# A fused two-layer transformer kernel: batch 0's routing moved forward, the expert steps split into five kinds, and batch 1's second bias formed on VectorE

## The chip, the cores and the metric

The program runs on one core of one Trainium2 chip. The metric is the device time of one execution in microseconds (us); lower is better. The kernel before takes 197.06 us, the median of three runs.

## The reference

Two samples (batches) of 512 tokens with 128 features pass through two cross-attention layers and two mixture-of-experts layers:

```python
x = x + L0_xcond(layernorm(x), ctx, ctx, tau, delta)   # 16 heads, 77 keys
x = x + L0_ffn(layernorm(x))                           # one shared FFN + an expert's LoRA
x = x + L1_xcond(layernorm(x), ctx, ctx, tau, delta)
x = x + L1_ffn(layernorm(x))                           # top-1 of 8 experts

def _L1_ffn_ref(x, switch_w, switch_b, w1, b1, w2, b2):
    t = x.reshape(-1, d)
    route_prob = softmax(t @ switch_w + switch_b)
    route_prob_max = max(route_prob); routes = argmax(route_prob)
    for e in range(8):
        h = gelu(t @ w1[e] + b1[e])          # 128 -> 512
        y = h @ w2[e] + b2[e]                # 512 -> 128
        out = where(routes == e, y, out)
    return out * route_prob_max
```

The change is in the last layer and in what leads up to it.

## The kernel before

The order of the work is written out by hand. `schedule()` (L107) holds a table of steps such as `sc/1/1/3` (kind / layer / batch / number), and each of the five engines walks through the same list and issues its own part of every step. So a step's place in the table sets its place in each engine's queue, and each engine runs its queue strictly in order; semaphores tie the engines together.

Steps that matter here:
- Attention: `max` (TensorE scores of a group, VectorE takes the row maximum, L965 and L756), `mt` (the maxima are transposed, L974, and copied by ScalarE and VectorE, L612 and L762), `sc` (scores on TensorE, L990, exponential on ScalarE, L620), `pv` (times the values, L1005), `rd` and `on` (reciprocal of the denominator on ScalarE, product on VectorE, L766), `wo` (output projection, L1012, and residual add on VectorE, L775).
- Routing of one batch: `ln/3` and `xn/3` (statistics and normalized rows, L690 to L708; in the last layer the reciprocal root is a `pow` on GpSimd, L500), `xt/3` (transposes, L917, and copy by ScalarE, L579), `route` (gate product, L1025, and the arg-max chain on VectorE, L786 to L796), `prob` (L810 to L816), `rank` (L1062, L1067; VectorE L841 to L850 gives each token its slot), `tiles` (L855 to L859, the expert of each tile, `tile_e`).
- GpSimd then scatters the batch's rows to the DRAM buffer `slots`, sorted by expert, with four indirect DMAs (L534). SyncE waits for all four and loads them back as 11 tiles of 128 rows in four DMAs (`LOADS`, L431).
- Expert steps: 22 tiles, 11 for each batch. In step `moe/t` TensorE transposes tile t+1 (L1091), forms the hidden layer of tile t (L1098, called H below) and the output of tile t-2 (L1109, called Y). ScalarE copies the transposed tile (`XST`, L659) and applies gelu (L666). VectorE copies the first weights of tile t+2's expert into one of `NWC` = 3 buffers (L871, called the weight copy: H of a tile waits for it), adds the gated second bias to tile t-1 (L879) and the result to tile t-2 (L884, called z). GpSimd forms the gated bias of a tile (`bias_of`, L479 to L492, buffer `PB`) and stores tile t-2 to `out` with an indirect DMA (L542).

Between the end of attention and the first tile TensorE runs `BRIDGE_X` = 14 products of constants (`keep_busy`, L903), whose result is not used. In the table `xt/3/1`, the transposes of batch 1, follows `moe/-1`, the transpose of tile 0:

```python
xn/3/1 moe/-1 xt/3/1 moe/0 route/1 moe/1 prob/1 rank/1 tiles/1
...
return steps + [("moe", t) for t in range(2, NS + 2)]
```

Of the kernel before, what the change touches and what calls it, by code (L numbers as in the profile page):

```python
# [57 lines left out]
NSB = NQ + E - 1  # L58
NS = B * NSB
# [5 lines left out]
BRIDGE_Q, BRIDGE_X = 14, 14  # L65
NHB = 3
NWC = 3
NPB = 6
AHEAD = NQ
# [37 lines left out]
def schedule():  # L107
# [50 lines left out]
def banks(steps):  # L158
# [22 lines left out]
def build(nc, x, ctx, att0, att1, consts, small, rows, ffn0w, loraB, sw, w1, b1, w2, b2, empty, out):  # L181
# [8 lines left out]
    with stages:  # L190
# [243 lines left out]
        def _(pool):  # L434
# [44 lines left out]
            def bias_of(n):  # L479
# [7 lines left out]
                if n >= NPB:  # L487
                    pool.wait_ge(based, n - NPB + 1)
# [3 lines left out]
                pool.tensor_tensor(PB[:, n % NPB], B2[:, bass.ds(e * D, D)], p, ALU.mult).then_inc(bias_ready, 1)  # L492
# [3 lines left out]
            for s in steps:  # L496
                if s[0] == "ln" and s[1] == 3:
                    b = s[2]
                    pool.wait_ge(var_ready, b + 1)
# [23 lines left out]
                elif s[0] == "rank":  # L523

                    b = s[1]
                    if b == 1:
                        bias_of(0)
                    pool.wait_ge(preset, 16)
                    pool.wait_ge(slot_ready, b + 1)
                    pool.wait_ge(p_ready, b + 1)  # L530
                    for i in range(b * NQ, (b + 1) * NQ):
                        if b == 1 and i > NQ:
                            bias_of(i - NQ)
                        pool.indirect_dma_start(slots, bass.IndirectOffsetOnAxis(ap=slot[:, i:i + 1], axis=0), ROW[:, i], None,  # L534
                                                bounds_check=NS * 128 - 1, oob_is_err=False).then_inc(rows_sent[b], 16)
                elif s[0] == "moe" and s[1] >= 2:

                    t = s[1] - 2
                    if t + AHEAD < NS:
                        bias_of(t + AHEAD)  # L540
# [671 lines left out]
```

## Time and profile before

| | us |
|---|---|
| median of 3 runs (197.03 to 198.96) | 197.06 |
| the profiled execution's own time | 196.75 |
| its span, first to last instruction | 194.9 |
| TensorE matmuls busy | 164.1 (84%) |
| VectorE busy | 122.1 (63%) |
| ScalarE busy | 97.4 (50%) |
| GpSimd busy | 75.5 (39%) |
| share of the chain that ended last: TensorE / VectorE / issue | 56% / 20% / 9% |

The profile comes from one execution of 196.75 us, whose span is 194.9 us. 1.85 us of its time lie around the span. Times in the trace count from the span's start. "Busy" for TensorE is the modelled time of its pipelined matmuls. The granted clock is given as a share of 2.4 GHz: 0.50 is the level of 1.2 GHz. What each engine waited for is in brackets behind a row.

### The profile page before, as it was taken

How to read it: one execution, taken by the hardware profiler on the slowest of the kernel's cores; microseconds unless marked ns; L12 is line 12 of the kernel's file. 1: busy time of each engine (PE TensorE's matmuls, PEld its weight loads, DVE VectorE, ACT ScalarE, POOL GpSimd, SP SyncE). 2: the span in 40 equal slices, each digit the busy share in tenths (PEclk: the TensorE clock that was granted, in tenths of full speed). 3: DMA queues.
4: the chain of work that ended last, by engine and by line, in shares of the span. 5: the costliest groups of instructions: out<-in, count | busy, mean ns of one | idle time of the engine just before them, and what ended most of it. 6: DMA issues, size and time to landing. Idle time of an engine off the chain costs nothing.

```text
span 194.9 us, 3393 instructions
## 1 busy us (share of the span) xinstructions
PE 164.1 (84%) x880; PEld 112.7 (58%) x881; DVE 122.1 (63%) x360; ACT 97.4 (50%) x228; POOL 75.5 (39%) x96
## 2 busy tenths in 40 slices
PE   7894699989988978678897989995678999999930
PEld 2542555646735733454573455633367999999920
DVE  2689845859663559977433998374567666655420
ACT  5392427845562363452327554465255576766700
POOL 8899160000400066020002001016204889888871
PEclk9999669999999999999999999999999999999996
DMA  6400007000000599940000000002640273100000
GB/s 189 159 3 4 4 5 246 6 0 3 5 4 7 143 330 405 531 171 0 3 0 0 0 0 0 0 3 97 180 138 31 82 194 123 32 18 10 22 26 2
DMA packets 14483, 15.48 MB, mean 79 GB/s; under 512 B 6842, under 2 KB 11205, under 8 KB 14400
## 3 DMA queue, kind: packets, MB, share of 16 engines
q1 hardware_dynamic: 12944, 13.29, 21.2%
q0 software_dynamic: 1088, 1.60, 2.5%
q10 hardware_dynamic: 432, 0.37, 0.7%
q8 instruction: 8, 0.13, 0.3%
q14 instruction: 11, 0.09, 0.2%
HBM read 13.50 MB, written 5.44 MB: 97 GB/s over the span
## 4 chain that ended last, share of the span: by engine, by line
PE 56%; DVE 20%; issue 9%; ACT 4%; POOL 4%; DMA 3%; POOLq 0%; SPq 0%; ACTq 0%; DVEq 0%
PE acc L1005 10%; PE scores L1098 9%; PE acc L1109 8%; PE scores L990 4%; PE shared L1052 4%; DVE MR L756 4%; DVE QG L746 4%; PE shared L965 3%; PE acc L903 3%; PE shared L1038 3%; PE shared L945 3%; POOL out L542 2%; PE shared L917 2%; PE shared L1025 2%; DVE XN L708 2%
## 5 line engine op out<-in xcount | busy, mean ns | idle before, releaser
L1005 PE MATMUL acc<-P,VP 123*128 123x512 f32 (+1 forms) x80 | 41.6, 620 | 0.6 <-ACT P L620 0.6
L620 ACT ACTIVATE P<-scores 123x512 f32<-123x512 f32 (+1 forms) x40 | 23.0, 595 | 22.3 <-PE scores L990 21.9
L666 ACT ACTIVATE HT<-scores,B 128x128 f32<-128x128 f32 x88 | 25.3, 369 | 12.7 <-PE scores L1098 10.0
L756 DVE TENSOR_REDUCE MR<-shared 128x4 f32<-128x308 f32 x64 | 26.8, 471 | 4.9 <-PE shared L965 4.5
L522 POOL TENSOR_TENSOR X<-X,ROWS 128x512 f32<-128x512 f32 x6 | 8.1, 1345 | 52.4 <-DVE XN L708 52.2
L990 PE MATMUL scores<-QG,KG 102*123 102x512 f32 (+1 forms) x48 | 23.1, 530 | 2.6 <-ACT QG L612 1.2
L542 POOL DMA_INDIRECT out<-XS,token x22 | 22.7, 1031 | 4.2 <-issue 4.0
L1098 PE MATMUL scores<-XST,HT 128*128 128x128 f32 x176 | 23.6, 277 | 0.8 <-ACT XST L659 0.8
L965 PE MATMUL shared<-KG,QG 98*128 98x308 f32 x64 | 21.5, 399 | 3.0 <-DVE MR L756 1.1
L1109 PE MATMUL acc<-W,HT 128*128 x176 | 23.1, 276 | 0.2 <-issue 0.2
L1098 PEld LDWEIGHTS scores<-XST,HT 128*128 128x128 f32 x176 | 21.4, 192 | 1.3 <-ACT XST L659 1.2
L1109 PEld LDWEIGHTS acc<-W,HT 128*128 128x128 f32 x176 | 21.3, 192 | 0.4 <-issue 0.4
L1005 PEld LDWEIGHTS acc<-P,VP 123*128 123x128 f32 (+1 forms) x80 | 14.6, 197 | 9.7 <-issue 7.4
L965 PEld LDWEIGHTS shared<-KG,QG 98*128 98x128 f32 x64 | 11.8, 195 | 11.3 <-issue 3.7
L746 DVE SCALAR_TENSOR_TENSOR QG<-shared,ATT,QG 32x512 fp32r<-32x512 f32 x16 | 11.9, 745 | 7.5 <-ACT QG L605 7.2
L871 DVE COPY HT<-W 128x512 f32 x22 | 10.2, 465 | 8.8 <-issue 7.4
L534 POOL DMA_INDIRECT slots<-ROW,slot x8 | 8.4, 1049 | 18.1 <-DVE slot L850 8.7
L513 POOL TENSOR_TENSOR KG<-Ks,CON 102x616 fp32r<-102x616 f32 x6 | 7.5, 1250 | 18.7 <-DVE Ks L723 18.3
L605 ACT ACTIVATE QG<-shared,ATT 64x512 fp32r<-64x512 f32 x16 | 10.9, 684 | 6.1 <-PE shared L945 5.8
L990 PEld LDWEIGHTS scores<-QG,KG 102*123 102x123 f32 (+1 forms) x48 | 8.4, 190 | 8.5 <-issue 5.4
L903 PE MATMUL acc<-idle 128*128 128x512 bf16 x40 | 11.8, 459 | 1.5 <-DVE idle L681 1.4
L492 POOL TENSOR_TENSOR PB<-B,XS 128x128 f32<-128x128 f32 x22 | 10.2, 465 | 2.7 <-issue 2.1
(121 smaller groups left out, 238.8 us busy)
## 6 DMA issues: line engine op xcount, KB each, us to landing
W<-in_w SPq DMA_DIRECT2D x16, 256.0 KB, 6.8
slots<-in_empty SPq DMA_DIRECT2D x1, 2860.0 KB, 14.2
XS<-slots SPq DMA_DIRECT2D x2, 650.0 KB, 6.1
XS<-slots SPq DMA_DIRECT2D x2, 390.0 KB, 4.2
W<-in_ffn0w SPq DMA_DIRECT2D x1, 534.0 KB, 4.5
XS<-slots SPq DMA_DIRECT2D x2, 260.0 KB, 2.7
X<-in_x SPq DMA_DIRECT2D x2, 256.0 KB, 4.1
B<-in_b SPq DMA_DIRECT2D x1, 512.0 KB, 4.3
```

The lines of the kernel that those rows point to most:

```text
L542: pool.indirect_dma_start(out, bass.IndirectOffsetOnAxis(ap=token[:, t:t + 1], axis=0), XS[:, t, 0:D], None, bounds_check=B * S - 1, oob_i ...
L605: act.activation(QG[0:64, b, g], bank(s)[r, :], ACT.Identity, bias=ATT[l][r, A_BQ + g:A_BQ + g + 1]).then_inc(qh_ready, 1)
L620: act.activation(P[0:w, n % NP], scores[n % 2][0:w, :], ACT.Exp).then_inc(probs_ready, 1)
L666: ins = act.activation(HG1[:, t % NHB, c], hidden[t % 2][:, c], ACT.Gelu_apprx_tanh, bias=B1[:, bass.ds(expert[t] * NF + k, 1)])
L746: dve.scalar_tensor_tensor(QG[64:96, b, g], bank(s)[64 * odd:64 * odd + 32, :], ATT[l][0:32, A_BQ + g:A_BQ + g + 1], QG[0:32, b, g].bitcas ...
L756: dve.tensor_reduce(MR[:, b, qt, g, 2:2 + HG], bank(s)[:, 0:GK].rearrange("p (h k) -> p h k", h=HG), AX.X, ALU.max).then_inc(max_read, 1)
L903: pe.matmul(acc[0][:, :], idle[:, 0:128], idle[:, 0:S], start=True, stop=True)
L965: pe.matmul(bank(s)[:, 0:GK], QG[0:ONES + 2, b, g, 128 * qt:128 * qt + 128], KG[0:ONES + 2, b, g, off:off + GK], start=True, stop=True).th ...
L990: ins = pe.matmul(scores[n % 2][0:w, :], KG[:, b, g, c:c + w], QG[:, b, g], start=(i == 0), stop=(i == len(parts) - 1))
L1005: pe.matmul(acc[half][:, :], VP[0:w, l, b, j, half], P[0:w, n % NP, :], start=(j == 0), stop=(j == NT - 1)).then_inc(probs_used, 1)
L1098: ins = pe.matmul(hidden[t % 2][:, 128 * k:128 * (k + 1)], W1C[:, t % NWC, 128 * k:128 * (k + 1)], XST[:, t % 2], start=True, stop=True)
L1109: ins = pe.matmul(acc[n % 2][:, 0:D], HG1[:, n % NHB, 128 * k:128 * (k + 1)], W2[:, bass.ds(expert[n] * (NF * D) + D * k, D)], start=(k == ...
```

## The change

The table of steps is rewritten from batch 1's second attention layer on, and the step `moe` is split into kinds with places of their own: `cw` (weight copy), `m1` (transpose of the next tile, H, gelu), `bs` (second bias), `m2` (Y and z), `pb` (bias formed on GpSimd) and `so` (store). `row` is one of the scatters that belonged to `rank`; `prob` has become the first part of `rank` on VectorE.

```diff
-NWC = 3
-NPB = 6
-AHEAD = NQ
+NPB = NSB
+NWC = 4
-BRIDGE_Q, BRIDGE_X = 14, 14
+BRIDGE_Q, BRIDGE_X = 14, 0
...
-        xn/3/1 moe/-1 xt/3/1 moe/0 route/1 moe/1 prob/1 rank/1 tiles/1
+        pv/1/1/9 rd/1/1/1 on/1/1/1 wo/1/1 m1/-1 pb/0:3 ln/3/1 m1/0 cw/2 m1/1 xn/3/1 bs/0 cw/3 m1/2 m2/0 xt/3/1 pb/3:6
+        bs/1 m1/3 so/0 route/1 cw/4 m2/1 pb/6 bs/2 rank/1 so/1 tiles/1 pb/7 m1/4 row/1/0 pb/8 row/1/1 pb/9 row/1/2 pb/10
+        row/1/3 m2/2 bs/3 cw/5
...
-    return steps + [("moe", t) for t in range(2, NS + 2)]
+    for t in range(5, NS + 3):
+        steps += [(kind, n) for kind, n in (("cw", t + 1), ("m1", t), ("bs", t - 1), ("m2", t - 2), ("pb", t + 4), ("so", t - 3))
+                  if n < NS and (kind != "pb" or NSB <= n < NPB)]
+    return steps
```

`NSB` is 11, so `NPB` = 11 means that GpSimd forms the gated bias for batch 0's tiles only. For batch 1 VectorE multiplies and adds in one instruction:

```diff
+                    if n < NPB:
                         dve.wait_ge(bias_ready, n + 1)
-                        dve.tensor_tensor(XS[:, n, 0:D], XS[:, n, 0:D], PB[:, n % NPB], ALU.add).then_inc(based, 1)
+                        dve.tensor_tensor(XS[:, n, 0:D], XS[:, n, 0:D], PB[:, n], ALU.add).then_inc(based, 1)
+                    else:
+                        dve.scalar_tensor_tensor(XS[:, n, 0:D], B2[:, bass.ds(expert[n] * D, D)], XS[:, n, R_P:R_P + 1],
+                                                 XS[:, n, 0:D], ALU.mult, ALU.add).then_inc(based, 1)
```

Batch 0's last reciprocal root goes from GpSimd's `pow` to ScalarE's Ln and Exp, as in the earlier layers; batch 1's stays on GpSimd:

```diff
-                if s[0] == "ln" and s[1] == 3:
+                if s == ("ln", 3, 1):
                     b = s[2]
-                    pool.wait_ge(var_ready, b + 1)
+                    pool.wait_ge(var_ready, 1)
...
-                    if st == 3:
+                    if (st, b) == (3, 1):
                         continue
```

**Batch 0's chain on TensorE**, from the second `mt` step of batch 1's attention to `route/0` (the gate product, L1025). Before:

```order
L974 MATMUL shared<-CON,MR 64x128 x4
L990 MATMUL scores<-QG,KG 123x512
L1005 MATMUL acc<-P,VP 128x512
L990 MATMUL scores<-QG,KG 123x512 x2
L1005 MATMUL acc<-P,VP 128x512
L990 MATMUL scores<-QG,KG 123x512
L917 MATMUL shared<-CON,ROW 128x128 x4
L1005 MATMUL acc<-P,VP 128x512
L1025 MATMUL shared<-SW,XNT 128x8 x4
```

Now:

```order
L917 MATMUL shared<-CON,ROW 128x128 x4
L1005 MATMUL acc<-P,VP 128x512
L965 MATMUL shared<-KG,QG 128x308 x2
L990 MATMUL scores<-QG,KG 123x512
L974 MATMUL shared<-CON,MR 64x128 x4
L1025 MATMUL shared<-SW,XNT 128x8 x4
```

The transposes of batch 0 (L917) have moved in front of `mt` (L974); `route/0` directly follows `mt`, and two `sc` and one `pv` that stood ahead of it come after it.

**The start of the expert steps on TensorE**, from batch 1's output projection (L1012). Before, with the bridge (L903) and batch 1's transposes (L917) right behind tile 0's (L1091):

```order
L1012 MATMUL shared<-ATT,OT 128x128 x4
L903 MATMUL acc<-idle 128x512 x14
L1085 TENSOR_LOAD tile_e
L1085 ISA x2
L1091 MATMUL shared<-CON,XS 128x128
L917 MATMUL shared<-CON,ROW 128x128 x4
```

Now:

```order
L1012 MATMUL shared<-ATT,OT 128x128 x4
L1083 TENSOR_LOAD tile_e
L1083 ISA x2
L1089 MATMUL shared<-CON,XS 128x128
L1083 TENSOR_LOAD tile_e
L1083 ISA x2
L1089 MATMUL shared<-CON,XS 128x128
L1096 MATMUL scores<-XST,HT 128x128 x4
```

The bridge is gone. Four tile transposes (L1089), three H (L1096) and the first Y now stand ahead of batch 1's transposes.

**VectorE at the end of batch 1's `tiles` step** (the last instruction writes `tile_e`). Before:

```order
L859 TENSOR_SCALAR tile_e<-tile_f 1x11
L868 TENSOR_LOAD tile_e
L868 ISA x2
L871 ISA
L871 COPY HT<-W 128x512
```

Now:

```order
L855 TENSOR_SCALAR tile_e<-tile_f 1x11
L884 SCALAR_TENSOR_TENSOR XS<-acc,XS 128x128
L873 CAST token<-XS 128x3
L876 TENSOR_TENSOR XS<-XS,PB 128x128
L864 TENSOR_LOAD tile_e
L864 ISA x2
L867 ISA
L867 COPY HT<-W 128x512
```

Before, the copy behind `tile_e` is tile 4's weights; now tile 4's copy stands ahead of `rank/1`, and behind `tile_e` come tile 2's z, tile 3's bias and then tile 5's weight copy.

On GpSimd the `pow` for batch 1 (`ln/3/1`) now stands behind `pb/0`, `pb/1` and `pb/2`, which wait for the first two loads; the four scatters of batch 1 have `pb/8` to `pb/10` between them where three other bias steps stood; and in the loop only stores are left.

## Rows read from the trace of the kernel before

**Rows 1.** windows of six stretches, columns in the first row.

```profile
core 0: us, PE busy (x) PEld busy (x) DVE busy (x) ACT busy (x) POOL busy (x), PEclk, DMA share, GB/s
14.00:20.50 6.50, 3.72 (x19) 2.18 (x17) 6.40 (x16) 1.62 (x1) 5.83 (x6) 1.00 0.07 4
20.50:27.30 6.80, 5.62 (x12) 2.85 (x11) 4.67 (x15) 2.17 (x5) 1.60 (x2) 0.50 0.07 5
66.00:71.00 5.00, 3.73 (x13) 1.79 (x12) 4.08 (x16) 3.60 (x8) 1.03 (x1) 1.00 0.96 279
131.60:139.40 7.80, 4.10 (x21) 2.26 (x22) 3.79 (x15) 2.50 (x3) 4.18 (x5) 1.00 0.34 107
139.40:152.56 13.16, 11.15 (x88) 9.79 (x89) 8.74 (x38) 7.75 (x28) 3.77 (x6) 1.00 0.36 112
152.56:186.66 34.10, 34.09 (x304) 33.90 (x303) 20.38 (x61) 22.45 (x84) 30.16 (x40) 1.00 0.23 67
```

**Rows 2.** timeline, batch 0's chain: start us, us, what, [idle before it <-releaser].

```profile
116.50 1.13 PE L1012 MATMUL shared<-ATT,OT 128*128 128x128 f32 x8
...
122.02 1.12 DVE L708 TENSOR_SCALAR ROW<-ROW,mean_var,rstd 128x128 f32<-128x128 f32 x4 [0.58 <-POOL rstd L500]
...
125.82 0.19 DVE L786 TENSOR_TENSOR lg<-shared,ROWS 128x32 f32<-128x32 f32 x1 [2.69 <-PE shared L1025]
```

**Rows 3.** chain that ended last, two pieces of TensorE's work in batch 1's attention.

```profile
120.77 0.86 PE acc L1005 x2
...
121.93 0.47 PE scores L990
```

**Rows 4.** timeline, end of attention to the first expert tile, TensorE and SyncE.

```profile
133.71 1.13 PE L1012 MATMUL shared<-ATT,OT 128*128 128x128 f32 x8 [2.16 <-DVE OT L766]
...
134.89 2.97 PE L903 MATMUL acc<-idle 128*128 128x512 bf16 x13
...
137.18 1.86 SPq L431 DMA_DIRECT2D XS<-slots  x4
...
139.40 0.33 PE L1091 MATMUL shared<-CON,XS 128*128 128x128 f32 x1 [1.54 <-DMA XS<-slots]
```

**Rows 5.** timeline, start of the expert phase, TensorE, ScalarE and GpSimd.

```profile
139.66 0.63 PE L917 MATMUL shared<-CON,ROW 128*128 128x128 f32 x4
...
139.77 0.28 ACT L659 ACTIVATE XST<-shared 128x128 f32<-128x128 f32 x1 [5.62 <-PE shared L1091]
...
140.38 0.41 POOL L492 TENSOR_TENSOR PB<-B,XS 128x128 f32<-128x128 f32 x1 [2.09 <-issue]
...
140.57 1.13 PE L1098 MATMUL scores<-XST,HT 128*128 128x128 f32 x8
...
141.54 0.96 PE L1025 MATMUL shared<-SW,XNT 128*128 128x8 f32 x8
...
141.85 1.14 ACT L666 ACTIVATE HT<-scores,B 128x128 f32<-128x128 f32 x4 [0.67 <-PE scores L1098]
```

**Rows 6.** timeline, VectorE from batch 1's routing to tile 4's weights.

```profile
142.53 0.19 DVE L786 TENSOR_TENSOR lg<-shared,ROWS 128x32 f32<-128x32 f32 x1 [0.57 <-PE shared L1025]
...
148.59 0.16 DVE L859 TENSOR_SCALAR tile_e<-tile_f 1x11 int32<-1x11 f32 x1
...
149.35 0.43 DVE L871 COPY HT<-W 128x512 f32 x1 [0.60 <-DVE tile_e L859]
```

**Rows 7.** timeline, TensorE at tiles 5 and 11, SyncE at batch 1's loads.

```profile
152.56 1.12 PE L1098 MATMUL scores<-XST,HT 128*128 128x128 f32 x8
...
156.45 1.85 SPq L431 DMA_DIRECT2D XS<-slots  x4
...
161.99 0.27 PE L1091 MATMUL shared<-CON,XS 128*128 128x128 f32 x1
```

**Rows 8.** timeline, the last result on VectorE and the last store on GpSimd.

```profile
186.94 0.35 DVE L884 SCALAR_TENSOR_TENSOR XS<-acc,XS 128x128 f32<-128x128 f32 x1 [0.79 <-PE acc L1109]
...
189.82 0.97 POOL L542 DMA_INDIRECT out<-XS,token  x1 [0.30 <-issue]
```

More of the change, by code:

```diff
@@ L152, in order @@
         nth[s] = counts[kind] = counts.get(kind, -1) + 1
-        if s[0] == "ln" and s[1] < 3:
+        if s[0] == "ln" and s[1:] != (3, 1):
             nth["act_ln", s[1], s[2]] = counts["act_ln"] = counts.get("act_ln", -1) + 1
@@ L165, in banks @@
         kind = s[0]
-        if kind == "moe":
+        if kind == "m1":
             rotation = 2
@@ L522, in _ @@
                     finish(pool.tensor_tensor(X[:, b], X[:, b], row, ALU.add), pre_added)
[L523 to L540, printed above, removed]
+                elif s[0] == "row":
+                    _, b, i = s
+                    if i == 0:
+                        pool.wait_ge(preset, 16)
+                        pool.wait_ge(slot_ready, b + 1)
+                        pool.wait_ge(p_ready, b + 1)
+                    i += b * NQ
+                    pool.indirect_dma_start(slots, bass.IndirectOffsetOnAxis(ap=slot[:, i:i + 1], axis=0), ROW[:, i], None,
+                                            bounds_check=NS * 128 - 1, oob_is_err=False).then_inc(rows_sent[b], 16)
+                elif s[0] == "pb":
+                    bias_of(s[1])
+                elif s[0] == "so":
+                    t = s[1]
                     pool.wait_ge(z_ready, t + 1)
@@ L836, in _ @@
                     b = s[1]
+                    dve.wait_ge(ex_ready, b + 1)
+                    if b == 1:
+                        link(dve.tensor_scalar(ex[:, b], ex[:, b], -1.0, 1.0, ALU.mult, ALU.add))
+                        link(dve.reciprocal(ex[:, b], ex[:, b]))
+                    link(dve.tensor_reduce(esum[:, b], ex[:, b], AX.X, ALU.add))
+                    if b == 1:
+                        link(dve.tensor_scalar(esum[:, b], esum[:, b], 2.0, -float(E), ALU.mult, ALU.add))
+                    dve.wait_ge(rows_set, 1)
+                    dve.reciprocal(ROW[:, b * NQ:(b + 1) * NQ, R_P], esum[:, b]).then_inc(p_ready, 1)
                     read(dve, s)
@@ L1070, in _ @@
                     ins.then_inc(full[use[s][0]], 1)
-                elif kind == "moe":
+                elif kind == "m1":
                     t = s[1]
                     if t == -1:
-                        for e in range(E):
-                            pe.wait_ge(in_w2[e], 16)
                         for i in (2, 3):
```

100 lines of the change are left out of this document (44 added, 56 removed).

## The prediction

> **What bounds the kernel now.** I read the windows first, because the kernel has stages with different limits. From 152.56 us to 186.66 us TensorE is busy for 34.09 of 34.10 us [rows 1]: this stage is TensorE's own work, 17 H and 19 Y groups and the transposes of tiles 7 to 21, and it shrinks only if something is taken from TensorE. Nothing is. So the change can gain or lose at three places: before 152.56, in the clock, and behind 186.66.
>
> The timeline shows those places. Batch 0's chain comes first: output projection on TensorE at 116.50, normalized rows on VectorE at 122.02 after GpSimd's `pow`, logits on VectorE at 125.82 [rows 2]. TensorE finishes attention at 134.84, fills 2.97 us with the bridge, and still waits 1.54 us for the first load before tile 0 at 139.40 [rows 4]. From there to H of tile 5 at 152.56 it is busy 11.15 of 13.16 us [rows 1, 7]. At the end VectorE writes the last z at 187.29 (186.94 + 0.35), but the last store starts at 189.82 [rows 8], because GpSimd is behind with its stores.
>
> **Batch 0's chain.** TensorE's output projection waited for VectorE, which had two row maxima and a copy ahead of the product; now the product comes first, and the reciprocal root no longer goes through GpSimd. So the normalized rows may come up to 2.7 us earlier than 122.02. But they are not what `route/0` waits for last: `mt` of the last maxima now stands right in front of it, and all TensorE work ahead of that. What has left the queue ahead of `route/0` is two `sc` at 0.47 and one `pv` at 0.86 [rows 3], 1.8 us; I expect about 0.9 us of new gaps there (TensorE waits for the product on VectorE, then the third `sc` waits for the first exponential). That leaves 0.9 us, between 0 and 2.7. All that follows (rank, scatters, SyncE's loads from 137.18 on [rows 4]) is a chain of its own and shifts with it. **Tile 0 is at 138.5 instead of 139.40.** TensorE's attention ends near 134.84 as before: the same products, and the two new weight copies on VectorE fit in its wait for the last reciprocal.
>
> **From tile 0 to H of tile 5.** This is the term I trust most, for it comes from the order. Before, batch 1's transposes came 0.26 us after tile 0's (139.40 to 139.66 [rows 4, 5]). Now three H and one Y stand ahead of them. Leg by leg:
> - tile 0 to its H, 139.40 to 140.57 [rows 4, 5]: 1.17
> - H to gelu, 140.57 to 141.85: 1.28. Then gelu 1.14 and the copy of tile 2's transpose 0.28, which ScalarE does in that order [rows 5], less 0.1 of overlap: 1.3
> - H of tile 2 and Y of tile 0: 34.10 us for 36 groups [rows 1] is 0.95 each, 1.9
> - batch 1's transposes to `route/1`, 139.66 to 141.54 [rows 5]: 1.9, with one H in it as before
> - `route/1` to the logits on VectorE, 141.54 to 142.53 [rows 5, 6]: 1.0
> - logits to the end of `tile_e`, 142.53 to 148.75 [rows 6]: 6.2, plus one z at 0.35 [rows 8]: 6.5. Tile 4's weight copy is in it as before
> - `tile_e` to H of tile 5. Before, the weight copy started 0.60 us later and took 0.43 [rows 6], 1.1 with the semaphore. Now one z, a cast and a bias add, small operations like the z, precede it, about 0.8 more: 1.9.
>
> The sum is 1.17 + 1.28 + 1.3 + 1.9 + 1.9 + 1.0 + 6.5 + 1.9 = 16.9 us, against 13.16. H of tile 5 starts at 138.5 + 16.9 = 155.4, which is **2.8 us later** than 152.56. TensorE has nothing to do in between: Y of tile 2 ends near 151.4 and H of tile 5 is next in its queue, held by the weight copy behind `tile_e`. That is a new wait of some 4 us. `pow` for batch 1, now behind three bias steps on GpSimd, is a parallel path: the first bias started 0.98 us after tile 0's load (139.40 to 140.38 [rows 4, 5]), so three end some 2.9 us after it, the rows follow about 2.2 us later, at 143.6, and TensorE comes to the transposes at 144.2. It is hidden by 0.6 us; if GpSimd takes longer for each, up to 1 us more is lost.
>
> After H of tile 5 everything is as before, one group behind the other. Batch 1's loads start at 156.45 [rows 7] plus the shift of `tile_e` (4.8 us), 161.3, and tile 11 is there 2.2 us later, as tile 0 was (137.18 to 139.40 [rows 4]), at 163.5; TensorE wants it at 161.99 [rows 7] + 2.8 = 164.8. It fits, by 1.3 us.
>
> **The stores.** GpSimd no longer forms 11 biases, 0.41 us each [rows 5] plus issue, so it keeps up. The last store then starts 0.7 to 1.5 us after the last z instead of 2.53 us (187.29 to 189.82 [rows 8]); it can't be at once, since three results come closer together than three stores of 0.97 us plus 0.30 can go [rows 8]. **Gain 1.5 us**, between 1.1 and 1.9. VectorE's combined instruction costs what a z costs, 0.35 us, a little more than the add; VectorE is busy 20.38 of 34.10 us [rows 1], so that is hidden. If it were not, 11 times 0.1 us would be lost.
>
> **The clock.** TensorE's granted clock is 1.00 in the stretch with the bridge [rows 1]. It fell to 0.50 (1.2 GHz) at 20.5 us after TensorE had been busy for 3.72 of 6.50 us, and came back at 27.3, after 5.62 us of busy time at the low level. With 3.73 of 5.00 us busy, at 66 to 71, it stayed up [rows 1]. Without the bridge TensorE does 1.13 us [rows 4] in the 6.9 us from 131.6 to 138.5. That is far below the stretch after which it fell, and so is the 4 us wait before tile 5. I expect the low level twice.
> - Before tile 0: what TensorE does in the path up to batch 1's transposes is 0.33 + 1.13 + 1.9, 3.4 us. All of it at half speed costs 3.4 more, none of it 0. Part of the low time passes while TensorE waits for ScalarE anyway; I take 1.2.
> - Before tile 5: there TensorE is the bound, and what is lost is half of the busy time at the low level, at most 5.62 / 2 = 2.8, at least 0. I take 1.3, since the low level will have begun in the wait.
>
> The Trainium skill says the same of such waits ("TensorE: Matmul & The Clock Gate", section "HAM oscillation — how this bites in real kernels"): a burst of matmuls, a wait for a transfer, and the next burst starts at half clock, each time anew. By it alone the sum would have both falls for certain, and a kernel that takes the bridge out loses by it. The trace agrees that the clock falls after sparse stretches, but the stretch at 66 to 71 us shows that not each wait does it.
>
> **The sum.** 2.8 (tile 5 later, which has the 0.9 of batch 0's chain in it) - 1.5 (stores) + 1.2 + 1.3 (clock) = +3.8 us. The span goes from 194.9 to 198.7 and the execution from 196.75 to 200.6. The profiled execution lies 0.3 us below the median of the runs; I leave that out. I predict 200.6 us.
>
> **Rivals.**
> - *The clock stays up, or falls at no cost.* Then only 2.8 - 1.5 = +1.3 is left: 198.1 us. For it: a low stretch can coincide with the wait. Against it: 1.13 us of work in 6.9.
> - *Faster: batch 0's loads land when attention ends.* If the first load is there by 134.9, TensorE goes on without a wait, the clock stays up, and H of tile 5 is at 134.9 + 16.9 = 151.8, 0.8 earlier than before; with the stores that is -2.3, 194.4 us. It needs batch 0's chain 4.5 us shorter; with the clock at no cost the kernel is faster than before once tile 0 is earlier than 138.5 - 1.3 = 137.2. The rows show 2.7 us at most for the normalized rows, and `route/0` has TensorE's queue in front. But my gaps are estimates, and a shorter chain also takes the clock's cost away.
> - *Batch 1 is late twice.* If `pow` and the bias steps take 1 us more and both falls cost most of their bounds, it is 200.6 + 1 + 1.5, about 203 us; tile 11 also comes too late once its 1.3 us are used up.
> - *GpSimd's relief is worth nothing*, because the last store waits for something else than GpSimd: then +1.5, 202.1 us. Against it: the stores at the end follow one another at 1.27 us without waiting for VectorE.
>
> **How the numbers follow.** A measurement of this kernel tells about 1% from no change, so faster is below 195.1 and slower above 199.0. The forecast has a chance of 0.45; the clock rival 0.27; the faster one 0.17; the two late ones 0.11 together. The forecast and the late ones are slower, 0.55 with a little taken off for a cheap clock; the clock rival is the same, 0.28; faster 0.17. The forecast's own range is 199 to 202.5. For 8 in 10 the range goes from 195.5, which leaves most of the faster case out, to 203.
>
> **What would show it.** Right: tile 0's transpose at 138 to 139 with an idle TensorE since 135, granted clock 0.50 right behind it; TensorE waiting 3 to 5 us for VectorE's weight copy of tile 5, at about 151 to 155; the last store 0.7 to 1.5 us after the last z. Wrong: tile 0 before 137, no wait at tile 5, or clock 1.00 throughout. The prediction as a whole is wrong if H of tile 5 starts before 153.

## The result, and the profile after

The changed kernel takes **203.26 us** (median of 4 runs, 202.73 to 205.04) against 197.05 us for the kernel before in the same session: ratio **1.032, interval 1.024 to 1.040**. It is slower by 6.2 us. The direction was forecast; the size was not: 200.6 had been said, and 203.26 lies just above the range, whose upper end was 203.0. A second session (run a0 below) gave 203.12 us and 1.036 (1.030 to 1.042). Below, a median is taken over all executions of a kernel, a ratio only over those within 1.5% of its fastest, which leaves out up to two of four (e3, e4, e11) and four of ten (h1).

The profiled execution is the slowest of the four: 205.04 us, span 202.9. This is the head of its page, with the row of the clock from its table of 40 slices:

```profile
span 202.9 us, 3306 instructions
PEclk9997579999999997999999999995899699999995
```

Each digit of PEclk is some 5 us. The 5 two thirds along the row (137 to 142 us) and the 6 behind it (157 to 162) are the two falls of the clock that the prediction wanted. The 7 before the middle (near 80 us) is a fall that neither the profile of before nor a0's has. It lies ahead of all the steps that were changed, and by 116 us this execution is 1.1 us behind a0's. The windows, in stretches that answer to [rows 1], show it in numbers:

```profile
131.60:139.60 8.00, 5.31 (x17) 2.99 (x15) 1.96 (x4) 3.70 (x5) 3.38 (x4) 0.82 0.32 101
139.60:156.60 17.00, 12.25 (x89) 11.10 (x89) 10.96 (x52) 8.17 (x29) 7.70 (x13) 0.88 0.23 73
156.60:196.00 39.40, 37.40 (x303) 35.78 (x303) 17.49 (x57) 22.74 (x83) 21.67 (x24) 0.96 0.21 65
```

From tile 0's transpose (139.6) to H of tile 5 (156.6) are 17.0 us; the prediction had 16.9, and 1.2 more for the clock; before it was 13.16. The surprise is the last row: 39.4 us for work that took 34.10 us before [rows 1]. The timeline of the end of attention, tile 0 and tile 5 answers to [rows 4 to 7]; its columns are start, duration, engine, line and operation, and in brackets the idle time before it with its releaser:

```profile
137.02 2.05 PE L1012 MATMUL shared<-ATT,OT 128*128 128x128 f32 x8 [2.16 <-DVE OT L765]
...
137.38 1.86 SPq L435 DMA_DIRECT2D XS<-slots  x4
...
139.62 0.48 PE L1089 MATMUL shared<-CON,XS 128*128 128x128 f32 x1 [0.56 <-DMA XS<-slots]
...
155.03 0.16 DVE L855 TENSOR_SCALAR tile_e<-tile_f 1x11 int32<-1x11 f32 x1
...
155.95 0.54 DVE L867 COPY HT<-W 128x512 f32 x1 [0.23 <-issue]
...
156.59 1.46 PE L1096 MATMUL scores<-XST,HT 128*128 128x128 f32 x8 [3.22 <-issue]
...
162.81 1.85 SPq L435 DMA_DIRECT2D XS<-slots  x4
```

The output projection of batch 1, the end of attention, starts at 137.02 instead of 133.71 [rows 4], of which 1.2 us are there before 116 us already, and runs at the low clock. H of tile 5 waits 3.22 us for the weight copy at 155.95, as forecast. Batch 1's tile numbers are 6.4 us later than before (155.03 against 148.59 [rows 6]), its loads too (162.81 against 156.45 [rows 7]).

Behind that comes what the prediction did not have. The stores of tiles 2, 3 and 4 (GpSimd, L541) go out with nothing between them, and the engines that read TensorE's results start long after these are recorded as done:

```profile
161.57 0.97 POOL L541 DMA_INDIRECT out<-XS,token  x1 [0.30 <-issue]
...
162.09 1.06 PE L1096 MATMUL scores<-XST,HT 128*128 128x128 f32 x8
...
162.85 0.97 POOL L541 DMA_INDIRECT out<-XS,token  x1 [0.30 <-issue]
162.98 1.06 PE L1108 MATMUL acc<-W,HT 128*128 x8
...
164.12 0.97 POOL L541 DMA_INDIRECT out<-XS,token  x1 [0.30 <-issue]
...
166.13 1.15 ACT L665 ACTIVATE HT<-scores,B 128x128 f32<-128x128 f32 x4 [3.28 <-PE acc L1108]
166.19 0.35 DVE L884 SCALAR_TENSOR_TENSOR XS<-acc,XS 128x128 f32<-128x128 f32 x1 [2.34 <-PE acc L1108]
...
167.50 0.70 PE L1096 MATMUL scores<-XST,HT 128*128 128x128 f32 x4 [1.46 <-ACT XST L658]
```

By the record H of tile 7 ended at 163.15 and Y of tile 5 at 164.04. ScalarE starts the gelu of tile 7 at 166.13, 2.98 us after the one, and VectorE z of tile 5 at 166.19, 2.15 us after the other; both engines were idle, and by the profile both waited for TensorE. Later it repeats in small. In steady state before, z started 0.11 us behind its Y. Now each second z is 0.7 us late:

```profile
171.43 0.97 POOL L541 DMA_INDIRECT out<-XS,token  x1 [1.74 <-DVE XS L884]
...
172.56 1.06 PE L1108 MATMUL acc<-W,HT 128*128 x8
172.81 0.99 POOL L541 DMA_INDIRECT out<-XS,token  x1 [0.41 <-issue]
...
174.38 0.35 DVE L884 SCALAR_TENSOR_TENSOR XS<-acc,XS 128x128 f32<-128x128 f32 x1 [1.43 <-PE acc L1108]
```

Y ends at 173.62, z starts at 174.38; two stores, 1.38 us apart, precede it. (Two z close together also bring the next two stores close together, so here the pairs are effect as well as possible cause.) The next weight copy is late by as much, the next H waits 0.2 to 0.3 us, and two tiles take 4.08 us instead of 3.79 (H of tile 11 at 171.60, of tile 13 at 175.68).

At the end the stores do keep up as forecast: last z at 196.01 + 0.35, last store at 197.85, 1.5 us later instead of 2.53:

```profile
196.01 0.35 DVE L884 SCALAR_TENSOR_TENSOR XS<-acc,XS 128x128 f32<-128x128 f32 x1 [0.62 <-PE acc L1108]
...
197.85 0.98 POOL L541 DMA_INDIRECT out<-XS,token  x1 [0.30 <-issue]
```

### The profile page after: what moved, and what is told of

Its sections match the earlier page's. It is cut to its first block and busy times, and to the rows that moved or that the text cites. A ratio compares the mean times of both kernels' runs of the same rounds, so it can differ in the third digit from the quotient of the medians.

```text
span 202.9 us, 3306 instructions
## 1 busy us (share of the span) xinstructions
PE 167.7 (83%) x867; PEld 117.5 (58%) x867; DVE 120.4 (59%) x359; ACT 98.8 (49%) x230; POOL 67.6 (33%) x84
## 5 line engine op out<-in xcount | busy, mean ns | idle before, releaser
L1096 PE MATMUL scores<-XST,HT 128*128 128x128 f32 x176 | 26.0, 295 | 5.3 <-issue 3.4
L541 POOL DMA_INDIRECT out<-XS,token x22 | 21.8, 993 | 23.7 <-DVE XS L884 18.5
L1096 PEld LDWEIGHTS scores<-XST,HT 128*128 128x128 f32 x176 | 23.4, 207 | 7.4 <-issue 5.2
L965 PE MATMUL shared<-KG,QG 98*128 98x308 f32 x64 | 23.1, 432 | 3.9 <-DVE MR L755 1.9
L990 PE MATMUL scores<-QG,KG 102*123 102x512 f32 (+1 forms) x48 | 24.0, 546 | 1.3 <-ACT P L619 0.8
L1108 PE MATMUL acc<-W,HT 128*128 x176 | 23.9, 283 | 0.0
L1108 PEld LDWEIGHTS acc<-W,HT 128*128 128x128 f32 x176 | 22.2, 198 | 0.0
L965 PEld LDWEIGHTS shared<-KG,QG 98*128 98x128 f32 x64 | 12.9, 213 | 12.5 <-issue 6.8
L884 DVE SCALAR_TENSOR_TENSOR XS<-acc,XS 128x128 f32<-128x128 f32 x22 | 7.6, 348 | 17.2 <-PE acc L1108 13.3
L903 PE MATMUL acc<-idle 128*128 128x512 bf16 x27 | 8.9, 501 | 1.4 <-DVE idle L680 1.4
```

The lines of the kernel that those rows point to most:

```text
L541: pool.indirect_dma_start(out, bass.IndirectOffsetOnAxis(ap=token[:, t:t + 1], axis=0), XS[:, t, 0:D], None, bounds_check=B * S - 1, oob_i ...
L965: pe.matmul(bank(s)[:, 0:GK], QG[0:ONES + 2, b, g, 128 * qt:128 * qt + 128], KG[0:ONES + 2, b, g, off:off + GK], start=True, stop=True).th ...
L990: ins = pe.matmul(scores[n % 2][0:w, :], KG[:, b, g, c:c + w], QG[:, b, g], start=(i == 0), stop=(i == len(parts) - 1))
L1096: ins = pe.matmul(hidden[t % 2][:, 128 * k:128 * (k + 1)], W1C[:, t % NWC, 128 * k:128 * (k + 1)], XST[:, t % 2], start=True, stop=True)
L1108: ins = pe.matmul(acc[n % 2][:, 0:D], HG1[:, n % NHB, 128 * k:128 * (k + 1)], W2[:, bass.ds(expert[n] * (NF * D) + D * k, D)], start=(k == ...
```

## The experiments

Times are medians; ratios are to the kernel before on the same chip, with their interval. A shift of one microsecond between single profiled executions means nothing: the low-clock stretch near 20 us varies in length (the mean granted clock of the first 40 us is 0.91 or 0.87), and some executions have a second one near 80 us. So I compare places within one execution, or two executions that are equally far at 115 us.

**a0: the changed kernel again.**

> The changed kernel once more, unaltered, to see which of its waits stand in every execution. If the long wait of tile 5 (TensorE idle 3.2 us behind tile 5's transpose), the low clock at 137 to 143.5 and at 157 to 160.5, and the 1.5 us wait of H of tile 9 for ScalarE at 166 to 167.5 come from the order, all of them are there again, each within 0.5 us. If the wait at tile 9 came from one disturbed execution, it is gone and the time is about 201.5 us. Time: 202.7 to 203.6 us.

203.12 us, 1.036 (1.030 to 1.042). Its profiled execution (span 200.5) is without the fall near 80 us (granted clock 1.00 from 78 to 82 us, 0.59 in the first one). VectorE's copy of the second maxima starts at 115.08 in it and at 114.95 in the kernel before, so the two can be compared, and it serves as the changed kernel's profile from here on:

```profile
138.40:155.90 17.50, 14.17 (x88) 13.07 (x89) 10.19 (x49) 8.25 (x29) 7.54 (x13) 0.74 0.23 73
155.90:167.10 11.20, 9.64 (x84) 9.45 (x85) 4.02 (x13) 4.33 (x16) 8.14 (x10) 1.00 0.48 145
167.10:193.50 26.40, 25.46 (x221) 24.61 (x220) 14.26 (x45) 17.89 (x68) 13.23 (x14) 1.00 0.11 35
```

Tile 0 is at 138.41, H of tile 5 at 155.91. From there to tile 11's transpose (167.1) it takes 11.2 us at full clock, of which TensorE works 9.64; before, 9.43 us (152.56 to 161.99 [rows 7]). So the stall of tiles 8 to 10 repeats.

**e1: the bridge back in.** **e2: tile 5's weight copy ahead of `rank/1`.** **e3: both.**

```diff
e1: -BRIDGE_Q, BRIDGE_X = 14, 0
e1: +BRIDGE_Q, BRIDGE_X = 14, 14
e2: - ... pb/6 bs/2 rank/1 so/1 tiles/1 ... m2/2 bs/3 cw/5
e2: + ... pb/6 bs/2 cw/5 rank/1 so/1 tiles/1 ... m2/2 bs/3
```

> Only BRIDGE_X goes back from 0 to 14. Theory (my clock term): the clock stays at 1.00 until tile 5, TensorE's first H takes 1.13 us instead of 1.92, and H of tile 5 comes 1.0 to 1.5 us earlier; the wait for tile 5 and the clock's fall there stay. 201.5 to 202.3 us. Rival: the low clock begins before the bridge, in the wait for the last reciprocal (it was at 0.50 from 136.9 on), so the 14 products run at half speed, delay tile 0, and cost as much as they give: 203 us or more.

> Only the weight copy of tile 5 is moved ahead of rank/1 on VectorE. Theory (tile 5 waits for the copy behind tile_e): TensorE goes from Y of tile 2 to H of tile 5 with under 0.5 us of idle time, the clock does not fall there, and the chain of batch 1 ends 0.8 us later (one copy). What is won there, 3.2 us and 1.7 us of clock, is partly given back where tile 6 or tile 11 now waits: 199 to 201.5 us. Rival: TensorE then waits at the next place of the same chain (the copy of tile 6, also behind tile_e), idle 3 us there, and nothing is won: 202.5 to 203.5 us.

> Both edits of e1 and e2. Theory: the two gains add, since one lies before tile 0 and the other at tile 5: the sum of what e1 and e2 gain against the changed kernel, within 0.5 us, about 198.5 to 200.5 us. Rival: the clock is one cause and the wait another of the same idle time, and the sum is less than the better of the two plus 0.5 us.

204.29 us, 1.039 (1.034 to 1.044); 204.11 us, 1.034 (1.026 to 1.041); 204.57 us, 1.032 (1.023 to 1.041). None helps. In e1 the bridge runs while the load lands, and tile 0 waits for the bridge instead. The clock now stays at 1.00 up to 157 us, but H of tile 5, which waits for batch 1's chain on VectorE, comes at 156.60 as in the first profile (156.59; the two are equally far at 116 us):

```profile
137.95 3.19 PE L903 MATMUL acc<-idle 128*128 128x512 bf16 x14
...
140.97 0.48 PE L1089 MATMUL shared<-CON,XS 128*128 128x128 f32 x2
```

In e2 H of tile 5 comes at 153.47 without a wait, but H of tile 6 then waits for the next copy, which is still behind `rank/1`:

```profile
157.54 1.77 PE L1096 MATMUL scores<-XST,HT 128*128 128x128 f32 x7 [2.01 <-issue]
```

**e4: the changed kernel with GpSimd forming batch 1's biases too.** (11 buffers, `n % NSB`, a wait for the buffer.)

```diff
-NPB = NSB
+NPB = NS
```

> The changed kernel, with batch 1's second bias formed on GpSimd as before and added on VectorE (order otherwise unchanged). Theory A (the slower stage after H of tile 5 comes from late signals of TensorE after a wait, and has nothing to do with the bias): the stall of some 3 us at tiles 8 to 10 is still there, the last store falls 2.5 us behind the last z instead of 1.5, and the time is 203.1 + 0.5 to 1.5 = about 204. Rival B (VectorE's longer bias at a dynamic address slows its loop to 4.08 us per two tiles): the pace goes back to 3.79 us per two tiles and the time falls to about 202.

Four runs: 200.65, 201.03, 209.1 and 404.37 us, so no interval. The first two are 3.0 us above the kernel before on this chip (197.83) and some 2.3 us under the changed kernel, where theory A had 204. In the profiled one TensorE is busy 19.98 of the 20 us from 160 to 180: the pace is back, as rival B had it. Two executions are a pointer only: the bias part seems to cost 2 us or more, where it was to bring 1.5.

**e5: the kernel before without its bridge.**

```diff
-BRIDGE_Q, BRIDGE_X = 14, 14
+BRIDGE_Q, BRIDGE_X = 14, 0
```

> The kernel before with its bridge of 14 idle matmuls after the end of attention left out, nothing else. Theory (what I priced at 1.2 us): the granted clock falls to 0.50 at the bridge's place and for about 6.5 us behind it, T of tile 0 starts at 139.4 as before, and the time is 196.8 + 1.2 to 2.5 = about 198.5. Rival (T0 waits for the loads anyway and the low stretch ends before much work is due): within 0.5 us of before.

198.48 us against 197.83, 1.003 (0.998 to 1.008). The interval holds both nothing and the 1.2 us of the theory. The granted clock from 134 to 140 us was 0.53 and from 140 to 150 0.67, so it fell, and in the profiled execution it did cost: from tile 0's transpose (139.74) to H of tile 5 (155.21) it takes 15.5 us, before 13.16.

**e6: the kernel before with the bias part of the change alone.**

```diff
-                    if t + AHEAD < NS:
+                    if t + AHEAD < NSB:
                         bias_of(t + AHEAD)
...
+                        else:
+                            dve.scalar_tensor_tensor(XS[:, n, 0:D], B2[:, bass.ds(expert[n] * D, D)], XS[:, n, R_P:R_P + 1],
+                                                     XS[:, n, 0:D], ALU.mult, ALU.add).then_inc(based, 1)
```

> The kernel before with one part of the change alone: batch 1's second bias multiplied and added by VectorE in one instruction, GpSimd forms it for batch 0 only. Theory (my term of -1.5 us): the last store starts 0.3 to 1.0 us behind the last z instead of 2.5, T and H unchanged, time 196.8 - 1.5 = about 195.3. Rival (GpSimd's relief is worth nothing since the stores catch up anyway): 196.8. Rival B of the run beside it: VectorE's loop gets slower, pace 4.08 us per two tiles in batch 1, time about 199.

199.71 us, 1.011 (1.006 to 1.017): the part that was to gain 1.5 us **loses 1.9 us** by the medians, in a kernel whose order is otherwise that of before. Theory and first rival missed; rival B named the time, but not the mechanism, for outside one stall the pace is still 1.9 us per tile. The profile shows the stall at the very place where GpSimd has its first stores without a bias between them:

```profile
165.65 1.06 PE L1113 MATMUL acc<-W,HT 128*128 x8
...
165.98 0.97 POOL L542 DMA_INDIRECT out<-XS,token  x1 [0.30 <-issue]
...
167.26 0.97 POOL L542 DMA_INDIRECT out<-XS,token  x1 [0.30 <-issue]
...
168.53 0.97 POOL L542 DMA_INDIRECT out<-XS,token  x1 [0.30 <-issue]
168.99 0.35 DVE L888 SCALAR_TENSOR_TENSOR XS<-acc,XS 128x128 f32<-128x128 f32 x1 [2.55 <-PE acc L1113]
```

Y ended at 166.71, its z starts at 168.99. That is the picture of tiles 7 to 9 of the changed kernel, but with batch 1's loads long done. From it came a **new theory S**: stores that GpSimd issues back to back, 1.27 to 1.4 us apart, make TensorE's results reach their readers late; the bias that GpSimd formed between two stores had kept them apart.

**e7: tile 5's and tile 6's copies ahead of `rank/1`.**

```diff
- ... pb/6 bs/2 rank/1 so/1 tiles/1 ... m2/2 bs/3 cw/5
+ ... pb/6 bs/2 cw/5 cw/6 rank/1 so/1 tiles/1 ... m2/2 bs/3
```

> The changed kernel with the weight copies of tiles 5 and 6 both ahead of rank of batch 1 on VectorE, so that no H waits for a copy between tiles 4 and 7. Theory A (late signals of TensorE begin with a wait of TensorE): H5 starts at about 153.5, H6 2 us later, no stall at tiles 8 to 10, pace 3.79; batch 1's loads land 1.2 us later, time about 199.5. Rival C (the stall comes with the transfers of batch 1, whatever TensorE did before): the stall of 3 us stays at 161 to 167 and the time is about 202.5. Rival D (rank pushed back by 1.2 us makes batch 1's loads late): T11 waits for the load, time about 203.

202.61 us, 1.030 (1.021 to 1.039); rivals C and D both. H of tile 5 starts at 151.13, but batch 1's loads now set the next point:

```profile
164.68 0.33 PE L1089 MATMUL shared<-CON,XS 128*128 128x128 f32 x1 [2.35 <-DMA XS<-slots]
```

**e8: the changed kernel with an idle multiply on GpSimd behind each store. e9: e6 with one ahead of each store that had a bias there before.** The cut shows e8's.

```diff
                     pool.indirect_dma_start(out, ...).then_inc(stored, 16)
+                    pool.tensor_tensor(spare, B2[:, 0:D], B2[:, 0:D], ALU.mult)
```

> The changed kernel, with one idle multiply of 128x128 on GpSimd behind each store (its result is used by nothing; everything else unchanged). New theory S (stores issued back to back, 1.27 to 1.45 us apart with nothing between them, hold back TensorE's signals to ScalarE and VectorE by 0.6 to 4 us; the bias that GpSimd formed between two stores kept them 1.7 us and more apart): the stall at tiles 8 to 10 shrinks to under 1 us, the pace of batch 1 is 3.79 us per two tiles, time about 200.0. Rival L (the stall is made by the loads of batch 1 or by TensorE's wait before them): stall and time unchanged, 203.1 or up to 0.5 more.

> The kernel before with VectorE forming and adding batch 1's second bias (the run that took 199.7), and on GpSimd one idle multiply of 128x128 at each place where a bias was formed before. Theory S: no stall in batch 1, time that of before, 197.0, within 0.5 us. Rival V (VectorE's two-input instruction with the dynamic address is what costs): 199.7 as without the idle multiplies.

e9: **197.18 us, 1.003 (0.999 to 1.008)**, against 199.71 and 1.011 for e6. An instruction whose result nobody reads, on a GpSimd that is now busier, takes the loss away. (The two intervals, from two chips, still touch between 1.006 and 1.008; g3 and g4 below, nearly the same kernel as e9, have 0.996 and 0.997.) VectorE's instruction is the same in both, so rival V is out. GpSimd and TensorE from 160 to 182 us, in e9 (columns: count, busy time with the mean of one, idle time ahead with its releasers):

```profile
L546 POOL DMA_INDIRECT out<-XS,token x14 | 14.3, 1022 | 2.3 <-issue 2.1 <-DVE XS L892 0.2
L1106 PE MATMUL scores<-XST,HT 128*128 128x128 f32 x93 | 12.5, 275 | 0.0
```

and in e6, where TensorE waits 2.4 us in the same stretch:

```profile
L1102 PE MATMUL scores<-XST,HT 128*128 128x128 f32 x82 | 11.2, 277 | 2.4 <-ACT XST L659 2.4
```

e8: 202.25 us, 1.028 (1.020 to 1.036), 0.9 us under a0 by the medians, on other chips. The stall is gone: TensorE is busy 11.38 of 11.50 us up to tile 11, and 24.81 of 25.00 behind it.

```profile
154.50:166.00 11.50, 11.38 (x85) 11.21 (x86) 5.33 (x15) 5.48 (x21) 9.90 (x14) 0.85 0.48 148
166.00:191.00 25.00, 24.81 (x220) 24.46 (x218) 14.09 (x44) 16.73 (x63) 19.49 (x27) 1.00 0.11 34
```

But the two stretches together take 36.5 us against 37.6 in a0, since the granted clock was 0.85 where a0 had 1.00: the low stretch came after the wait for tile 5's copy instead of ahead of it. In the changed kernel the stall's end is seen in the trace, while its worth in time, about 1 us, lies within the intervals.

e8 and e9 ran in one session, and both have VectorE's biases and spaced stores. What is left between them is the new order of the steps, with the bridge out and the small changes that belong to it: 202.25 against 197.18 us, **5.1 us**. By this pair most of the 6.2 us lie there.

**e10: three stores back to back in the kernel before**, far from any load, the biases on GpSimd as before.

```diff
+                    if t in (13, 14):
+                        continue
                     pool.wait_ge(z_ready, t + 1)
-                    pool.indirect_dma_start(out, ... token[:, t:t + 1] ...)
+                    for n in (13, 14, 15) if t == 15 else (t,):
+                        pool.indirect_dma_start(out, ... token[:, n:n + 1] ...)
```

> The kernel before, GpSimd's biases as they were, but the stores of tiles 13 and 14 held back and issued together with that of tile 15, three with nothing between them, far from any load. Theory S: TensorE's signals around tiles 17 and 18 reach the other engines 1 to 3 us late, and the time is 197.0 + 1 to 2.5 = about 198.7. Rival L (a load of batch 1 must be in flight too): unchanged, 197.0 within 0.5.

**198.42 us, 1.008 (1.004 to 1.012)** against 196.87: one such burst costs 1.5 us.

```profile
178.12 1.01 POOL L545 DMA_INDIRECT out<-XS,token  x1 [0.16 <-issue]
...
179.06 1.06 PE L1112 MATMUL acc<-W,HT 128*128 x8
...
179.43 0.97 POOL L545 DMA_INDIRECT out<-XS,token  x1 [0.30 <-issue]
179.96 0.27 PE L1094 MATMUL shared<-CON,XS 128*128 128x128 f32 x1
...
180.70 0.97 POOL L545 DMA_INDIRECT out<-XS,token  x1 [0.30 <-issue]
...
182.46 0.35 DVE L887 SCALAR_TENSOR_TENSOR XS<-acc,XS 128x128 f32<-128x128 f32 x1 [2.71 <-PE acc L1112]
182.49 0.28 ACT L662 ACTIVATE XST<-shared 128x128 f32<-128x128 f32 x1 [1.85 <-remote]
182.82 1.16 PE L1101 MATMUL scores<-XST,HT 128*128 128x128 f32 x8 [0.80 <-issue]
```

Y ends at 180.12, T at 180.23; their readers start at 182.46 and 182.49, 2.3 us later. Before the burst the same two steps took 0.1 to 0.25 us. No load is in flight, so rival L is out. That the spacing of the stores matters is shown by three runs: the burst makes the delay (e10), taking the spacing away makes it (e6), and giving the spacing back removes it (e9). By what path it does so, none of them shows.

**e11: the changed kernel with before's order at the end of attention. g2: with before's order of the expert steps, and the idle multiply.**

```diff
e11: -... wo/1/0 sc/1/1/0:3 ln/3/0 ... route/0 pv/1/1/3 sc/1/1/5 rank/0 pv/1/1/4 rd/1/1/0 sc/1/1/6 tiles/0 row/0/0:4 ...
e11: +... wo/1/0 sc/1/1/2 ... ln/3/0 ... xt/3/0 pv/1/1/4 route/0 sc/1/1/7:9 rd/1/1/0 pv/1/1/5 rank/0 pv/1/1/6 tiles/0 row/0/0:4 ...
g2:  -... ln/3/1 m1/0 cw/2 m1/1 xn/3/1 bs/0 cw/3 m1/2 m2/0 xt/3/1 ... route/1 cw/4 ... rank/1 ...
g2:  +... ln/3/1 xn/3/1 m1/-1 xt/3/1 cw/2 m1/0 route/1 cw/3 m1/1 bs/0 rank/1 tiles/1 pb/0 row/1/0 ...
```

> The changed kernel with the order of before in the last quarter of attention (batch 0's chain not ahead; the expert part and the bias as changed, no bridge). Theory (moving batch 0's chain ahead costs the end of attention 2.0 us and gives tile 0 nothing): the last pv ends at 131.6, T0 starts at about 139.4 when the load has landed, time within 1 us of 203.1, since the later start is hidden. Rival (the chain ahead is worth the 0.9 us I gave it): 204.0.

> The changed kernel's attention (batch 0's chain ahead, no bridge) and its bias on VectorE, but the expert steps in the order of before (batch 1's transposes and routing right behind tile 0, rank behind H1) and one idle multiply on GpSimd behind each store. Theory (the order of the five kinds costs the H5 wait): T0 at 138.4, no H waits over 0.5 us behind tile 5, last H as in before or 1 us earlier, time 196.0 to 197.5. Rival (the attention's end, 2 us later, and the low clock behind it weigh as much): 199.

e11: 206.51 us (203.61 to 207.44); g2: 204.29 us, 1.034 (1.025 to 1.043). Both expectations missed: both kernels are slower than expected. In e11 tile 0 starts at 141.40, 3.0 us later than in a0. Some 1.4 us of that are there at 116 us already, ahead of the part that differs; the other 1.6 us or so are what moving batch 0's chain ahead gives tile 0. In g2 TensorE stands from tile 0's transpose (138.33) until batch 1's rows are there (142.68), because attention now ends 2.2 us later. So neither half of the new order, put back alone, brings time back; both put back, as in e9, do.

**g1: e7 and the idle multiply together.**

> The changed kernel with both mends together: weight copies of tiles 5 and 6 ahead of rank of batch 1, and one idle multiply on GpSimd behind each store. If theory S is whole and the copies were the rest: H5 at about 153 and H6 without a wait, the wait for tile 7's copy of some 1 to 2 us at most, no stall at tiles 8 to 10, time about 199.5. Rival (the wait only moves on to the next copy, whatever is done): 202, as with the idle multiply alone.

202.05 us, 1.024 (1.016 to 1.032). TensorE waits 2.34 us for batch 1's first load (transpose of tile 11 at 164.87) and then runs at the low clock. What binds here is batch 1's own chain.

**h1: the kernel before, batch 1's loads held back as late as in the changed kernel. h2: the same in e6.**

```diff
                 sp.wait_ge(rows_sent[b], 16 * NQ)
+                if b == 1:
+                    sp.wait_ge(z_ready, 8)
```

> The kernel before with one wait more: SyncE starts batch 1's loads only behind the eighth z (about 162.9, 6.4 us later than now, and as late as in the changed kernel). Theory: T of tile 11 starts at 164.8 instead of 161.99, TensorE idles 2.8 us for it, the granted clock may fall behind that, and the time is 197.0 + 2.8 to 4.5 = about 200.5. Rival (the loads' lateness is hidden, the loss lies elsewhere in the order of the steps): 197.0 to 198.

> Both causes together in the kernel before: batch 1's loads behind the eighth z, and batch 1's bias on VectorE with GpSimd's stores back to back. If the causes add: 197.0 + 3.5 + 2.5 = about 203, the time of the changed kernel. If the late loads hide the stores' effect (the same stretch pays once): about 201.

h1: 199.48 us (ten runs, 197.57 to 202.09) against 196.62, 1.5% by the medians and 1.007 (1.003 to 1.012) by the ratio. In the profiled one tile 11 comes as forecast:

```profile
162.84 1.85 SPq L433 DMA_DIRECT2D XS<-slots  x4
...
164.97 0.33 PE L1093 MATMUL shared<-CON,XS 128*128 128x128 f32 x1 [2.80 <-DMA XS<-slots]
```

h2: 201.51 us, 1.023 (1.016 to 1.030), 4.9 us more by the medians. That is about the sum of the two alone (1.9 in e6, 2.9 in h1), and less than the 6 us of the changed kernel.

**g3 and g4: e9 without the idle multiply ahead of the last three stores.**

```diff
-                    if t >= NSB - AHEAD:
+                    if NSB - AHEAD <= t < NS - 3:
```

> The kernel before with batch 1's bias on VectorE and idle multiplies between the stores (197.2), but none ahead of the last three stores. If stores may go back to back there, since few signals of TensorE are left to hold back: the last store starts 1.2 us earlier and the time is 196.0. Rival (they hold back the last H and Y): 197.2 or more.

> The kernel before with batch 1's bias on VectorE, idle multiplies between the stores and none ahead of the last three, as g3, which came out at 0.996 of before (0.992 to 1.001). Theory (the last store starts 1.2 us earlier at nearly no price): 0.995, the interval below 1. Rival (chance of the runs): 1.000.

196.78 us, 0.996 (0.992 to 1.001), and 196.56 us, 0.997 (0.993 to 1.001). Both intervals hold 1. With its side effect taken away, moving the bias to VectorE may be worth 0.3 or 0.4%, at most 0.8% by the intervals; no version here is shown to beat the kernel before.

## Why the prediction was wrong, point by point

I compare a0's profiled execution (span 200.5) with that of before (194.9), +5.6 us, against +3.8 predicted. The prediction had two parts: the order and the clock, 2.8 + 1.2 + 1.3 = +5.3 us, and the stores, -1.5 us. The first came out at +5.1 us by e8 against e9 (at +3.0 by the two executions of e4). **The second failed in its sign:** taking the biases off GpSimd was to bring 1.5 us and costs 1.9 (e6), because it also took away what kept the stores apart.

- **Batch 0's chain.** Said: tile 0 at 138.5. Measured: 138.41. Right, though one assumption beside it failed: "TensorE's attention ends near 134.84 as before". The output projection of batch 1 started at 135.90 in a0, 2.2 us behind 133.71 [rows 4]. It did no harm to tile 0, which waited for its load anyway, but it pushed batch 1's chain (seen in g2).
- **From tile 0 to H of tile 5, with the clock before tile 0.** Said: 16.9 + 1.2 = 18.1 us. Measured: 17.5, against 13.16. The wait for the weight copy is where it was said to be. Undoing it (e2, e7) does not pay, since the next copy and then batch 1's load take its place.
- **The clock.** Said: low twice, 1.2 and 1.3 us. It did fall twice, right behind tile 0 and around tile 5; in a0 the second fall lay ahead of H of tile 5 (1.79 us for H of tile 4), and then H of tile 5 and all after it ran at 1.00. So the 1.3 us is not where it was put, in the work behind H of tile 5. The 1.2 us before tile 0 is neither shown nor refuted: without the bridge the kernel before loses between -0.2 and 0.8% (e5), and in the changed kernel the bridge gives nothing back (e1), since H of tile 5 waits for batch 1's chain either way. No run takes the fall at tile 5 away alone.
- **"After H of tile 5 everything is as before, one group behind the other."** This is where the failed step shows in the trace. Said: 34.10 us, plus 1.3 for the clock. In a0, 11.2 us instead of 9.43 to tile 11 and 26.4 instead of 24.67 behind it, +3.5 us, all at full clock. For 2.5 of these TensorE stood idle (11.20 - 9.64 and 26.40 - 25.46), where before it stood for 0.01 us, and the waits begin behind the stores at 160.97, 162.29 and 163.57. The idle multiply takes this idle time down to 0.3 us (11.38 busy of 11.50, 24.81 of 25.00). So the idle time comes from the stores' spacing; that the execution gets shorter by as much is not shown, for in e8 the low clock took half of it back. The margin of 1.3 us for tile 11's load was nearly right: its loads start at 162.22 in a0 (161.3 was said), and as soon as TensorE is earlier (e7, g1) it waits for them.
- **The stores: the step that failed.** Said: "Gain 1.5 us", since GpSimd keeps up. The last store does follow 1.5 us after the last z (before 2.53), so a gain of 1.0 is there. But the same relief takes the spacing out of the stores. Alone, the part costs 1.9 us instead of bringing 1.5 (e6), and in the changed kernel some 2.3 us (a0 against the two executions of e4). I had taken GpSimd's bias as load only; it was also what kept the stores 1.69 us apart, as in the kernel before:

```profile
160.66 1.05 POOL L542 DMA_INDIRECT out<-XS,token  x1 [0.16 <-issue]
161.73 0.46 POOL L492 TENSOR_TENSOR PB<-B,XS 128x128 f32<-128x128 f32 x1
...
162.35 1.05 POOL L542 DMA_INDIRECT out<-XS,token  x1 [0.16 <-issue]
```

The sum for a0: -1.0 (tile 0) + 4.3 (to tile 5) + 3.5 (behind it) - 1.2 (stores at the end, last Y to last store) = +5.6 us. Predicted, in the same places: -0.9, +4.9, +1.3, -1.5. Three terms are within 0.6 us; the one that was not worked out leg by leg made the miss. Another 0.3 us lie outside the span (202.65 - 200.5 against 196.75 - 194.9).

Of the rivals, "batch 1 is late twice" gave the right time, about 203, for another reason: it had `pow` and the clock. "GpSimd's relief is worth nothing" had the right sign for its term, but not the size.

What stays open: with stores spaced and copies early (g1) the changed kernel is still 2.4% slower (1.6 to 3.2). h1 shows that late loads of batch 1 alone cost a part of that in the kernel before, 0.7% by the ratio and 1.5% by the medians, and TensorE's wait for them is seen in g1 and e7. How much of the 2.4% is that and how much the clock, the runs don't separate. The two estimates of what the order costs also differ: 5.1 us (e8 against e9), but 3.0 us in the two executions of e4.

## What to carry to other kernels

When work is taken from an engine, ask what that work did for the timing of the instructions around it; an engine that is relieved, and so issues its indirect DMAs faster, is not free. When signals of one engine seem late to all of its readers at once, look at what another engine issues in that stretch, and test it by a burst in a quiet place of the old kernel and an idle instruction in the new one. And a stage that is "as before" needs its own row in the sum: check there each resource that the change touches.

## What the runs showed of the hardware

Indirect stores from GpSimd, 128 rows of 512 bytes, issued 1.27 to 1.35 us apart while TensorE works, make the readers of its results start 2 to 3 us late (e6, e10, a0 and the first profile). At 1.37 to 1.44 us apart, in pairs (the first profile, from tile 9 on), they are 0.7 us late. At 1.6 us (e8, e9) TensorE hardly waits, and at 1.69 us (before) it does not. One burst of three costs 1.5 us of time (e10). The spacing alone is not enough, though. The last five stores of the kernel before are 1.27 to 1.31 us apart, from 184.68 on, and its last z starts at 186.94 [rows 8], 0.28 us behind the last Y (183.74 + 2.92 = 186.66). There TensorE has no further group behind it:

```profile
183.74 2.92 PE L1109 MATMUL acc<-W,HT 128*128 x24
...
184.68 1.01 POOL L542 DMA_INDIRECT out<-XS,token  x1 [0.17 <-issue]
...
185.99 0.97 POOL L542 DMA_INDIRECT out<-XS,token  x1 [0.30 <-issue]
```

ScalarE and VectorE are late together, each with a signal of its own from TensorE. The ends of matmuls are modelled in the record, so the trace doesn't tell whether TensorE itself was held up or only its signals came late; its next groups are recorded as started on time (H of tile 8 at 163.98 and Y of tile 6 at 164.88 in the first profile, while the readers of H of tile 7 and Y of tile 5 waited until 166.13). The Trainium skill names one thing that can hold an engine back ("NOTIFIC — the notification-queue block", section "7.1 Overflow: three behaviours, one of which stalls the engine"): the block that carries the engines' records holds a producer back when its inner queues are full, rather than lose a record. No run here shows that block, and the cause stays open. Each execution timed here has a recorded span and clock, so no run tells either whether the delay is there when nothing is recorded.

The granted clock was low behind TensorE's longer waits in the expert part: behind 3.22 us at tile 5 in the first profile, 2.01 us at tile 6 in e2, and 2.80 us at tile 11 in h1 (0.76 from 164 to 171 us). It stayed at 1.00 behind the 2.16 us wait of the output projection before [rows 4], where the bridge followed. What a fall costs varied with what lay in the low stretch: 2.3 us between tile 0 and H of tile 5 in e5, nothing at H of tile 5 in the changed kernel (e1).
